# One stationary tile for gate and up of the shared expert, and a SiLU that writes to other partitions

## The chip, the cores and the metric

The kernel runs on one core of one Trainium2 chip. The metric is the device time of one execution in microseconds (us). The kernel before takes 1531.22 us, the median of three runs from 1531.09 to 1531.66.

## The reference, cut to what matters

A macaron block on x of shape (8, 512, 128), all in fp32:

```
x = x + 0.5 * ffn(layernorm(x))
x = x + (layernorm(x) + attention(layernorm(x)))
x = x + 0.5 * ffn(layernorm(x))

ffn(h):      # the same weights both times
    routed   = sum over e of cw[t,e] * ((silu(h @ w_gate[e]) * (h @ w_up[e])) @ w_down[e])   # 32 experts, 64 hidden each
    shared   = (silu(h @ shared_w_gate) * (h @ shared_w_up)) @ shared_w_down                 # 64 hidden
    anchor   = the same form, 16 anchors with 32 hidden each, one anchor per token
    return routed + shared + 0.1 * anchor
```

The combine weights `cw` come from a sigmoid router with a top-2 choice of groups and a top-6 choice of experts. The kernel computes all experts densely and multiplies by `cw`.

## The kernel before

The 4096 tokens are cut into 8 chunks of 512. Each of the two feed-forward blocks (`ffn`, here FFN 1 and FFN 2) goes through the 8 chunks, so there are 16 chunks in all. The hidden columns of all experts (2048), anchors (512) and the shared expert (64) are laid side by side and cut into `HT` = 21 tiles of 128. Tile 20, the last, holds only the 64 columns of the shared expert; its other 64 columns are zeros, in the gate weights, the up weights and the down rows.

For each tile j of a chunk g:

- TensorE (`gate_up`, from L361) multiplies the 128 weight columns by the 512 tokens into one PSUM bank for gate (`psG`) and one for up (`psU`). An fp32 product is made of three matmuls with fp32r halves (`mm3`, L196 to L198: hi by hi, hi by lo, lo by hi), so a tile takes three matmuls for gate and three for up. Every one has a moving operand of 512 columns.
- ScalarE (L725) writes `silu` of the gate bank to SBUF, one of two buffers.
- VectorE (L1069) multiplies it by the up bank into `gated`, one of three buffers, and then (L1097) by the combine weights of the tile's experts, spread over the partitions by a DMA, into `z`. For tile 20 the second step is a plain multiplication by 0.5 (L1100), into a `z` buffer of its own.
- TensorE (`down`, L374) multiplies the rows of `w_down` by `z` and accumulates over the 21 tiles in one bank. It is a plain fp32 matmul, which the trace shows as two records. It runs `LAG` = 3 tiles behind: `down` of tile 17 follows `gate_up` of tile 20, and those of tiles 18, 19 and 20 follow `gate_up` of tiles 0, 1 and 2 of the next chunk.

Each engine runs its own instruction list in a fixed, hand-written order, and semaphores join them. Around the end of a chunk TensorE's order is: `gate_up` 19, `down` 16, `gate_up` 20, `down` 17, `gate_up` 0 of the next chunk, `down` 18, `gate_up` 1, `down` 19, four transposes of the next normalised chunk (`prep_xT`, L336, which wait for `xn_ready`), `gate_up` 2, `down` 20. `gate_up` of a tile waits for `gated` of the tile three before. VectorE's order is: `gated` 19, in FFN 1 the row statistics of a finished chunk (L905, L907), `z` 19, `gated` 20, in FFN 1 the mean and variance (L913 to L919), `z` 20, the normalisation of the chunk after next (`normalise`, L924), `gated` 0, `z` 0. In the first chunk of each FFN a Newton step for the reciprocal standard deviation (`finish_std`, L884 to L895) stands between `z` 20 and the normalisation, and ScalarE computes the square root for it after `silu` 20.

After the last chunk of FFN 1 TensorE does `down` 18 and 19, then waits for `a_xT_lo` (VectorE, L1132, which stands behind `z` 20), projects keys and queries of the first attention pair, and only then does `down` 20. After the last chunk of FFN 2 it does `down` 18, 19 and 20 in a row, and then the chunk's output is copied, transposed, added and stored.

The weights are loaded once, in three groups of seven tiles, and split into their halves by ScalarE (L703) and GpSimd (L1267).

Of the kernel before, what the change touches and what calls it, by code (L numbers as in the profile page):

```python
# [23 lines left out]
ALU = mybir.AluOpType  # L24
# [44 lines left out]
def build(nc, x_in, wg_in, wu_in, wd_in, gate_in, bias_in, wq_in, wk_in, wv_in, wo_in,  # L69
# [6 lines left out]
    with ctx:  # L76
        def sb(name, shape, dt=F32):
            return ctx.enter_context(nc.sbuf_tensor(name, shape, dt))
# [15 lines left out]
        gate_w = sb("gate_w", [P, E])  # L94
        bias = sb("bias", [P, E])
        wg = [sb(f"wg_{n}", [P, HC], F32R) for n in ("hi", "lo")]
        wu = [sb(f"wu_{n}", [P, HC], F32R) for n in ("hi", "lo")]
        wd = sb("wd", [P, HC])
        stage = sb("stage", [P, 2, 3, GT * P])
        stage_flat = stage[:, :, :, :].rearrange("p a b c -> p (a b c)")  # L100
# [125 lines left out]

        ROUTE = 37

        def pair(b, p):

            return b * HP + p
# [25 lines left out]
        @block.sync  # L257
        def _(sp):
            def load_group(sp, k):
                cols = slice(k * GT * P, (k + 1) * GT * P)  # L260
                for w, src in enumerate((wg_in, wu_in)):
                    sp.dma_start(stage[:, k % 2, w, :], src[:, cols]).then_inc(w_loads[k], 16)
                sp.dma_start(wd[:, cols], wd_in[:, cols]).then_inc(w_loads[k], 16)

            def load_x(sp, c):
                sp.dma_start(x[:, c * TB:(c + 1) * TB, :],
                             x_in[c * CH:(c + 1) * CH, :].rearrange("(t p) d -> p t d", p=P)) \
                    .then_inc(x_loads[c], 16)

            sp.dma_start(small[:, :], small_in).then_inc(s["consts_loaded"], 16)  # L270
            load_x(sp, 0)
            sp.dma_start(gate_w[:, :], gate_in).then_inc(s["consts_loaded"], 16)
            sp.dma_start(bias[:, :], bias_in.partition_broadcast(P)).then_inc(s["consts_loaded"], 16)
            load_group(sp, 0)
            load_x(sp, 1)
            load_group(sp, 1)
            for c in range(2, NC):
                load_x(sp, c)
            for k in range(2, W_GROUPS):

                sp.wait_ge(wsplit[k - 2], 2)
                load_group(sp, k)

            def spread_weights(g, first, store=None, after_attention=False):

                sp.wait_ge(s["cwT_sb"], g + 1)
                rows = cw_rows[bass.ds((g % 2) * ROWS, ROWS), :] if not isinstance(g, int) else \
                    cw_rows[(g % 2) * ROWS:(g % 2 + 1) * ROWS, :]
                sp.dma_start(rows, cwT[:, :]).then_inc(s["cw_stored"], 16)
                sp.wait_ge(s["cw_stored"], 16 * (g + 1))  # L290
                if after_attention:
                    sp.wait_ge(s["out_ps"], NC * HP)
                for j in range(SPREAD_TILES):
                    if not (first and j < NSPREAD):
                        sp.wait_ge(s["z_done"], g * HT + j + 1 - NSPREAD - (1 if j < NSPREAD else 0))
                    n = P // (MI if j < E * MI // P else AI)
                    row = j * 2 if j < E * MI // P else E + (j - E * MI // P) * n
                    row = (g % 2) * ROWS + row
                    src = cw_rows[row:row + n, :] if isinstance(g, int) else \
                        cw_rows[bass.ds(row, n), :]  # L300
                    sp.dma_start(spread[:, j % NSPREAD, :],
                                 src.unsqueeze(0).broadcast_to([P // n, n, CH])) \
                        .then_inc(spread_loads[j % NSPREAD], 16)
                    if j == 11 and store is not None:
                        store_chunk(store)

            def store_chunk(c):

                sp.wait_ge(s["x_added"], (c + NC) + 1)
                sp.dma_start(out[bass.ds(c * CH, CH), :].rearrange("(t p) d -> p t d", p=P),  # L310
                             x[:, bass.ds(c * TB, TB), :]).then_inc(s["stored"], 16)

            spread_weights(0, True)

            for k in range(W_GROUPS):
                sp.wait_ge(wsplit[k], 2)
            for w, src in enumerate((wq_in, wk_in)):
                sp.dma_start(attn_w[:, w, :], src).then_inc(s["attn_w_loaded"], 16)
            sp.dma_start(wo[:, :].rearrange("p (j d) -> p j d", d=P),
                         wo_in.rearrange("(j p) d -> p j d", p=P)).then_inc(s["attn_w_loaded"], 16)  # L320
            sp.dma_start(attn_w[:, 2, :], wv_in).then_inc(s["attn_w_loaded"], 16)
            with sp.Fori(1, NC) as g:
                spread_weights(g, False)
            spread_weights(NC, False, after_attention=True)
            with sp.Fori(NC + 1, 2 * NC) as g:
                spread_weights(g, False, g - 1 - NC)
            store_chunk(NC - 1)
            sp.wait_ge(s["stored"], 16 * NC)
# [3 lines left out]
        def _(pe):  # L332
# [24 lines left out]
            def gate_up(g, j, first):  # L357
                if j == 0:
                    pe.wait_ge(s["xT_lo"], g + 1)
                if not (first and j < 3):  # L360
                    pe.wait_ge(s["gated_done"], tiles(g, j) - 3)  # L361
                c = slice(j * P, (j + 1) * P)
                xp = [of_chunk(t, g) for t in xT_parts]
                mm3(pe, psG[j % 3], [w[:, c] for w in wg], xp, True, True)
                mm3(pe, psU[j % 3], [w[:, c] for w in wu], xp, True, True) \
                    .then_inc(s["gate_up_ps"], 1)

            def down(g, j, first):
                pe.wait_ge(s["z_done"], tiles(g, j))
# [298 lines left out]
        def _(act):  # L668
# [28 lines left out]

            def split_hi(k, ws=range(2)):
                act.wait_ge(w_loads[k], 48)
                c = slice(k * GT * P, (k + 1) * GT * P)  # L700
                for w in ws:
                    dst = (wg, wu)[w]
                    nc.scalar.activation(dst[0][:, c], stage[:, k % 2, w, :], ACT.Copy) \  # L703
                        .then_inc(wsplit_hi[k], 1)

            def ffn_chunk(g, first, last, std_n=None):
                for j in range(HT):
                    if std_n == 2 and j in SPLIT_LAST:
                        split_hi(2, (SPLIT_LAST.index(j),))
                    if j == XT + 2 and not last:  # L710
                        prep_copy(g + 1)
                    if j == CWT + 1 and not last:
                        prep_cwT(g + 1)
                    if j == LOGITS + 1 and not last:
                        prep_sigmoid(g + 1)
                    if std_n == 3 and j == 12:
                        row_std(3)
                    if std_n == 3 and j >= AW_SLOT and j - AW_SLOT < 3:
                        attn_split_hi(j - AW_SLOT)
                    if std_n == 3 and j == HT - 1:  # L720
                        a_xT_high(0, psM)
                    act.wait_ge(s["gate_up_ps"], tiles(g, j))
                    if not (first and j < 2):
                        act.wait_ge(s["gated_done"], two_ago(g, j))
                    nc.scalar.activation(silu[j % 2], psG[j % 3], ACT.Silu) \  # L725
                        .then_inc(s["silu_done"], 1)
                    if j == 2 and not first:
                        y_copy(g - 1)
                if first:
                    row_std(std_n)  # L730
# [147 lines left out]
        def _(dve):  # L878
# [181 lines left out]
            def ffn_chunk(g, g0, first, last):  # L1060
# [3 lines left out]
                for j in range(HT):  # L1064
                    if j == 0 and not last:
                        dve.wait_ge(s["xT_ps"], g + 1)
                        normalise(g + 1 - g0, "xn_ready")
                    dve.wait_ge(s["silu_done"], tiles(g, j))
                    tt(gated[j % 3], psU[j % 3], silu[j % 2], ALU.mult) \  # L1069
                        .then_inc(s["gated_done"], 1)  # L1070
                    if j == 9 and not first:
                        add_y(g - 1, g0)
                    if j == XT + 3 and not last:
# [23 lines left out]
                        tt(z[part_slot(j)], gated[j % 3], spread[:, j % NSPREAD, :], ALU.mult) \  # L1097
                            .then_inc(s["z_done"], 1)
                    else:
                        nc.vector.tensor_scalar(z[part_slot(j)], gated[j % 3], 0.5, None, ALU.mult) \  # L1100
                            .then_inc(s["z_done"], 1)
                if before_attention:
                    a_xT_low(0, psM)
# [142 lines left out]
            normalise(0, "xn_ready")  # L1246
            nc.vector.tensor_copy(half[:, :], small[:, P:7 * P])
            nc.vector.memset(cw[:, :, ROWS:], 0.0)
            xT_low(0)
            for k in ROUTING:  # L1250
                ROUTING[k](0)
# [9 lines left out]
        @block.gpsimd  # L1261
        def _(pool):
            def split_lo(k, w):
                c = slice(k * GT * P, (k + 1) * GT * P)
                dst = (wg, wu)[w]
                pool.wait_ge(wsplit_hi[k], w + 1)
                nc.gpsimd.tensor_tensor(dst[1][:, c], stage[:, k % 2, w, :], f32(dst[0][:, c]),  # L1267
                                        ALU.subtract).then_inc(wsplit[k], 1)

            for w in range(2):  # L1270
# [79 lines left out]
```

## Time and profile before

| | |
|---|---|
| median of three runs | 1531.22 us |
| the profiled execution's own time | 1531.53 us |
| span of its trace, first to last instruction | 1529.7 us |
| TensorE busy | 1457.3 us, 95% of the span |
| VectorE busy | 1072.6 us, 70% |
| ScalarE busy | 813.9 us, 53% |
| GpSimd busy | 293.5 us, 19% |
| mean granted clock of TensorE | 0.994 of full speed |

FFN 1 takes the span from about 33 to 432 us, attention from there to about 1129 us, and FFN 2 the rest. A line of the timeline gives the start, the duration, the engine, the line of the kernel, and the operation. Records of matmuls overlap: the duration of one includes its way through the array, and the next starts before it ends. What a matmul takes from the next is the distance between their starts. VectorE's and ScalarE's records can overlap by a little as well.

### The profile page before, as it was taken

What the parts mean: (1) busy time and instruction counts of PE and PEld (TensorE: products, weight loads), DVE (VectorE), ACT (ScalarE), POOL (GpSimd) and SP (SyncE); (2) the same over time, 40 slices, a digit from 0 to 9 for tenths busy, and PEclk for the clock granted to TensorE, in tenths of its full rate; (3) what the DMA queues carried; (4) which work ended last, traced back from release to release, by engine and by line L of the source; (5) the groups of instructions that cost most, each with busy time, mean ns of one, the idle gap of its engine ahead of it and who ended that gap; (6) DMA issues with size and microseconds to landing.
All of it is one profiled execution on the core that took longest, in us unless ns stands there. A gap on an engine that the chain in (4) does not pass through costs nothing.

```text
span 1529.7 us, 29784 instructions
## 1 busy us (share of the span) xinstructions
PE 1457.3 (95%) x9664; PEld 973.4 (64%) x9664; DVE 1072.6 (70%) x2413; ACT 813.9 (53%) x1912; POOL 293.5 (19%) x589
## 2 busy tenths in 40 slices
PE   2999999999989999999999999999889999999998
PEld 1666666666655666665666666666556666666665
DVE  6977877788666666666666575666568777777775
ACT  3444333433457777777777677777743344333422
POOL 2100000000114434334344344344310000000000
PEclk9999999999999999999999999999999999999999
DMA  5443333333300000000000000000023333333333
GB/s 180 130 164 110 106 103 113 105 112 95 113 21 1 1 2 2 2 1 3 2 2 1 3 1 3 1 1 1 1 72 107 111 126 103 118 105 123 106 122 85
DMA packets 58867, 97.94 MB, mean 64 GB/s; under 512 B 6144, under 2 KB 15360, under 8 KB 58752
## 3 DMA queue, kind: packets, MB, share of 16 engines
q1 hardware_dynamic: 58752, 96.44, 19.9%
q8 instruction: 68, 1.11, 0.3%
q14 instruction: 47, 0.39, 0.1%
HBM read 92.75 MB, written 3.67 MB: 63 GB/s over the span
## 4 chain that ended last, share of the span: by engine, by line
PE 49%; issue 30%; POOL 16%; DVE 4%; DMA 1%; ACT 0%; POOLq 0%; SPq 0%; DVEq 0%
PE banks L374 17%; POOL work L1291 16%; PE banks L196 9%; PE banks L198 9%; PE banks L197 9%; PE banks L336 1%; PE banks L346 1%; DVE work L1097 1%; DVE work L1069 1%; PE banks L503 0%; POOL pool_pace L1286 0%; DVE bn L907 0%; DMA bias<-in_gate_bias 0%; DMA work<-cw_rows 0%; POOL aw_lo L1280 0%
## 5 line engine op out<-in xcount | busy, mean ns | idle before, releaser
L725 ACT ACTIVATE work<-banks 128x512 f32<-128x512 f32 x336 | 200.5, 597 | 462.4 <-PE banks L198 444.2
L374 PE MATMUL banks<-work,wd 128*128 128x512 f32 x672 | 342.9, 593 | 0.3 <-DVE work L1097 0.3
L1069 DVE TENSOR_TENSOR work<-banks,work 128x512 f32<-128x512 f32 x336 | 231.9, 690 | 153.0 <-ACT work L725 148.1
L780 ACT ACTIVATE work<-banks,nmax 128x512 f32<-128x512 f32 (+3 forms) x512 | 263.7, 526 | 39.3 <-DVE nmax L1153 39.2
L1291 POOL TENSOR_SCALAR work<-work,rrec 128x512 f32<-128x512 f32 (+3 forms) x512 | 261.6, 533 | 1.6
L196 PE MATMUL banks<-xT_hi,wg_hi 128*128 (+1 forms) x336 | 247.9, 738 | 0.0
L1097 DVE TENSOR_TENSOR work<-work 128x512 f32<-128x512 f32 x320 | 225.7, 705 | 15.8 <-DVE work L1069 9.3
L1168 DVE COPY stage<-banks 128x1024 f32<-128x1024 f32 (+1 forms) x128 | 122.0, 953 | 128.0 <-PE banks L489 128.0
L1153 DVE TENSOR_REDUCE nmax<-banks 128x2 f32<-128x1024 f32 (+3 forms) x256 | 196.0, 808 | 6.4 <-PE banks L478 6.3
L374 PEld LDWEIGHTS banks<-work,wd 128*128 128x128 f32 x672 | 126.3, 189 | 33.4 <-issue 2.2
L196 PE MATMUL banks<-xT_hi,wu_hi 128*128 (+1 forms) x336 | 133.3, 397 | 0.0
L197 PE MATMUL banks<-xT_lo,wg_hi 128*128 (+1 forms) x336 | 133.3, 397 | 0.0
L198 PE MATMUL banks<-xT_hi,wu_lo 128*128 (+1 forms) x336 | 133.3, 397 | 0.0
L197 PE MATMUL banks<-xT_lo,wu_hi 128*128 (+1 forms) x336 | 133.3, 397 | 0.0
L198 PE MATMUL banks<-xT_hi,wg_lo 128*128 (+1 forms) x336 | 133.1, 396 | 0.0
L791 ACT ACTIVATE stage<-banks 128x512 f32<-128x512 f32 x128 | 76.5, 597 | 105.0 <-PE banks L489 105.0
L489 PE MATMUL banks<-small,work 64*128 64x64 f32 x2560 | 111.6, 223 | 3.0 <-DVE stage L1168 2.4
L468 PE MATMUL banks<-k_hi,q_hi 64*128 64x256 f32 (+2 forms) x512 | 102.3, 396 | 8.0 <-ACT work L780 4.2
L196 PEld LDWEIGHTS banks<-xT_hi,wg_hi 128*128 128x128 f32 x336 | 64.1, 191 | 66.7 <-issue 63.8
L197 PEld LDWEIGHTS banks<-xT_lo,wg_hi 128*128 128x128 f32 x336 | 64.5, 192 | 65.2 <-issue 64.8
L780 ACT ACTIVATION_READ_ACCUMULATOR work<-banks,nmax 128x1 f32 x512 | 105.3, 206 | 0.0
L1142 DVE SCALAR_TENSOR_TENSOR q_lo<-banks,q_hi 128x512 fp32r<-128x512 f32 x64 | 44.3, 692 | 85.5 <-ACT q_hi L758 85.4
(122 smaller groups left out, 2215.0 us busy)
## 6 DMA issues: line engine op xcount, KB each, us to landing
work<-cw_rows SPq DMA_DIRECT2D x320, 256.0 KB, 3.1
x<-in_x SPq DMA_DIRECT2D x8, 256.0 KB, 7.0
out_rows<-x SPq DMA_DIRECT2D x8, 256.0 KB, 2.2
cw_rows<-cwT SPq DMA_DIRECT2D x16, 96.0 KB, 1.9
stage<-in_w_gate SPq DMA_DIRECT2D x3, 448.0 KB, 5.7
stage<-in_w_up SPq DMA_DIRECT2D x3, 448.0 KB, 6.4
wd<-in_w_down SPq DMA_DIRECT2D x3, 448.0 KB, 7.3
stage<-in_wq SPq DMA_DIRECT2D x1, 512.0 KB, 3.8
```

Of the source, the lines that this page charges most:

```text
L196: pe.matmul(o, w[0], m[0], start=start, stop=False, skip_group_check=True)
L197: pe.matmul(o, w[0], m[1], start=False, stop=False, skip_group_check=True)
L198: return pe.matmul(o, w[1], m[0], start=False, stop=stop, skip_group_check=True)
L374: pe.matmul(psY, wd[:, j * P:(j + 1) * P], z[part_slot(j)], start=j == 0, stop=j == HT - 1, skip_group_check=True).then_inc(s["down_ps"], 1)
L489: m = pe.transpose(psT[:, h, k * DK:(k + 1) * DK], prob[r, p % 2, i, o:o + P], ident[r, h * DK:(h + 1) * DK])
L725: nc.scalar.activation(silu[j % 2], psG[j % 3], ACT.Silu) \
L780: m = nc.scalar.activation(prob[:, p % 2, i, o:o + w], ps[:, i, so:so + w], ACT.Exp, bias=nmax[:, p % 2, i, qb:qb + 1], accum_out=rsum[:, ...
L1069: tt(gated[j % 3], psU[j % 3], silu[j % 2], ALU.mult) \
L1097: tt(z[part_slot(j)], gated[j % 3], spread[:, j % NSPREAD, :], ALU.mult) \
L1153: m = nc.vector.tensor_reduce(nmax[:, p % 2, :, qb], ps[:, :, o:o + (qb + 1) * P], AX.X, ALU.max, negate=True)
L1168: nc.vector.tensor_copy(*transposed(p, g, slice(0, 2 - g))).then_inc(s["pT_dve"], 1)
L1291: nc.gpsimd.tensor_scalar(t, t, rrec[:, par, i, qb:qb + 1], 1.0, ALU.mult, ALU.mult) \
```

## The change

The shared expert's up columns move into the 64 free columns of the gate weights of tile 20. The three gate matmuls of tile 20 then give 64 gate rows (partitions 0 to 63) and 64 up rows (partitions 64 to 127) in one bank, and the three up matmuls of tile 20 are gone. ScalarE reads partitions 0 to 63 of the bank and writes the SiLU to partitions 64 to 127 of its buffer; VectorE multiplies it by the up rows on partitions 64 to 127, and scales them by 0.5 there. The down rows of the shared expert move to the upper half of their tile, and the lower half of the `z` buffer is set to zero once at the start. The up weights are one tile narrower, so the third group's load and split of the up weights cover six tiles, not seven.

```diff
-        wu = [sb(f"wu_{n}", [P, HC], F32R) for n in ("hi", "lo")]
+        wu = [sb(f"wu_{n}", [P, HC - P], F32R) for n in ("hi", "lo")]
...
+        def split_columns(k, w):
+
+            return slice(k * GT * P, min((k + 1) * GT, HT - w) * P)
...
                 for w, src in enumerate((wg_in, wu_in)):
-                    sp.dma_start(stage[:, k % 2, w, :], src[:, cols]).then_inc(w_loads[k], 16)
+                    c = split_columns(k, w)
+                    sp.dma_start(stage[:, k % 2, w, 0:c.stop - c.start], src[:, c]).then_inc(w_loads[k], 16)
...
-                mm3(pe, psG[j % 3], [w[:, c] for w in wg], xp, True, True)
-                mm3(pe, psU[j % 3], [w[:, c] for w in wu], xp, True, True) \
-                    .then_inc(s["gate_up_ps"], 1)
+                m = mm3(pe, psG[j % 3], [w[:, c] for w in wg], xp, True, True)
+                if j < HT - 1:
+                    m = mm3(pe, psU[j % 3], [w[:, c] for w in wu], xp, True, True)
+                m.then_inc(s["gate_up_ps"], 1)
...
-                    nc.scalar.activation(silu[j % 2], psG[j % 3], ACT.Silu) \
-                        .then_inc(s["silu_done"], 1)
+                    if j < HT - 1:
+                        nc.scalar.activation(silu[j % 2], psG[j % 3], ACT.Silu) \
+                            .then_inc(s["silu_done"], 1)
+                    else:
+                        nc.scalar.activation(silu[j % 2][MI:, :], psG[j % 3][0:MI, :], ACT.Silu) \
+                            .then_inc(s["silu_done"], 1)
...
-                    tt(gated[j % 3], psU[j % 3], silu[j % 2], ALU.mult) \
-                        .then_inc(s["gated_done"], 1)
+                    if j < HT - 1:
+                        tt(gated[j % 3], psU[j % 3], silu[j % 2], ALU.mult) \
+                            .then_inc(s["gated_done"], 1)
+                    else:
+                        tt(gated[j % 3][MI:, :], psG[j % 3][MI:, :], silu[j % 2][MI:, :], ALU.mult) \
+                            .then_inc(s["gated_done"], 1)
...
-                        nc.vector.tensor_scalar(z[part_slot(j)], gated[j % 3], 0.5, None, ALU.mult) \
+                        nc.vector.tensor_scalar(z[part_slot(j)][MI:, :], gated[j % 3][MI:, :], 0.5, None,
+                                                ALU.mult) \
                             .then_inc(s["z_done"], 1)
...
             nc.vector.memset(cw[:, :, ROWS:], 0.0)
+            nc.vector.memset(z[part_slot(HT - 1)][0:MI, :], 0.0)
             xT_low(0)
```

The rest of the diff passes the narrower column ranges to the two splits and lays out the weights on the host.

## Rows read from the trace of the kernel before

**Rows 1.** The page: busy time of each engine and its share of the span.
```profile
PE 1457.3 (95%) x9664; PEld 973.4 (64%) x9664; DVE 1072.6 (70%) x2413; ACT 813.9 (53%) x1912; POOL 293.5 (19%) x589
```

**Rows 2.** Windows: length, busy time of PE, PEld, DVE, ACT, POOL; clock; DMA.
```profile
180.00:240.00 60.00, 60.00 (x229) 40.78 (x227) 46.05 (x127) 22.96 (x35) 0.00 (x0) 1.00 0.34 112
...
1220.00:1280.00 60.00, 60.00 (x229) 40.79 (x228) 44.40 (x105) 23.27 (x36) 0.00 (x0) 1.00 0.35 112
```

**Rows 3.** Waits of the span: total us, times, longest us.
```profile
PE banks L336 <- DVE xn L924: 12.4, 2, 11.5
```

**Rows 4.** The page's groups: last up matmul; busy us, mean ns, idle before.
```profile
L198 PE MATMUL banks<-xT_hi,wu_lo 128*128 (+1 forms) x336 | 133.3, 397 | 0.0
```

**Rows 5.** Timeline of TensorE, FFN 1, tile 20 of a middle chunk, and the next transposes.
```profile
231.43 0.39 PE L196 MATMUL banks<-xT_hi,wu_hi 128*128 x1
...
231.89 0.39 PE L198 MATMUL banks<-xT_hi,wu_lo 128*128 x1
232.12 1.02 PE L374 MATMUL banks<-work,wd 128*128 128x512 f32 x2
...
237.50 0.60 PE L336 MATMUL banks<-small,xn 128*128 128x128 f32 x4
```

**Rows 6.** Timeline of VectorE at the same boundary, from z 19 on.
```profile
232.15 0.67 DVE L1097 TENSOR_TENSOR work<-work 128x512 f32<-128x512 f32 x1
232.95 0.69 DVE L1069 TENSOR_TENSOR work<-banks,work 128x512 f32<-128x512 f32 x1
...
234.34 0.43 DVE L1100 TENSOR_SCALAR work<-work 128x512 f32<-128x512 f32 x1
235.11 1.12 DVE L924 TENSOR_SCALAR xn<-x,mean,rstd 128x128 f32 x4 [0.34 <-issue]
```

**Rows 7.** Timeline from the first to the second chunk of FFN 1.
```profile
84.05 0.69 DVE L1097 TENSOR_TENSOR work<-work 128x512 f32<-128x512 f32 x1
...
84.65 0.69 DVE L1069 TENSOR_TENSOR work<-banks,work 128x512 f32<-128x512 f32 x1
...
87.38 1.13 DVE L924 TENSOR_SCALAR xn<-x,mean,rstd 128x128 f32 x4 [0.51 <-DVE rstd L895]
...
88.67 0.60 PE L336 MATMUL banks<-small,xn 128*128 128x128 f32 x4
```

**Rows 8.** Timeline from FFN 1 to attention.
```profile
429.40 2.74 PE L374 MATMUL banks<-work,wd 128*128 128x512 f32 x6
429.42 0.69 DVE L1097 TENSOR_TENSOR work<-work 128x512 f32<-128x512 f32 x1
...
430.23 0.69 DVE L1069 TENSOR_TENSOR work<-banks,work 128x512 f32<-128x512 f32 x1
...
431.30 0.68 DVE L1132 TENSOR_TENSOR xT_lo<-banks,xT_hi 128x512 fp32r<-128x512 f32 x1
432.04 0.50 PE L196 MATMUL banks<-xT_hi,aw_hi 128*128 128x512 f32 x1
```

**Rows 9.** Timeline of a middle boundary of FFN 2: normalisation and transposes.
```profile
1426.17 1.13 DVE L924 TENSOR_SCALAR xn<-x,mean,rstd 128x128 f32 x4 [0.31 <-issue]
...
1429.26 0.60 PE L336 MATMUL banks<-small,xn 128*128 128x128 f32 x4
```

**Rows 10.** Timeline of the end of FFN 2: down 17 to 20, and z 20.
```profile
1521.35 3.60 PE L374 MATMUL banks<-work,wd 128*128 128x512 f32 x8
...
1522.90 0.43 DVE L1100 TENSOR_SCALAR work<-work 128x512 f32<-128x512 f32 x1
```

**Rows 11.** Timeline: a ScalarE copy on 48 partitions, and VectorE's idle time at the start.
```profile
228.75 0.59 ACT L692 ACTIVATE cwT<-banks 48x512 f32<-48x512 f32 x1 [0.78 <-PE banks L336]
...
13.82 0.69 DVE L1050 TENSOR_TENSOR xT_lo<-xT,xT_hi 128x512 fp32r<-128x512 f32 x1 [1.52 <-ACT xT_hi L678]
```

**Rows 12.** Windows at the end of attention, columns as in rows 2.
```profile
1113.00:1121.00 8.00, 7.34 (x50) 3.32 (x48) 3.34 (x19) 0.81 (x2) 4.07 (x9) 0.57 0.00 1
1121.00:1128.00 7.00, 5.99 (x46) 2.84 (x40) 4.01 (x10) 2.84 (x6) 0.00 (x0) 1.00 0.01 2
```

More of the change, by code:

```diff
@@ L699, in split_hi @@
                 act.wait_ge(w_loads[k], 48)
-                c = slice(k * GT * P, (k + 1) * GT * P)
                 for w in ws:
+                    c = split_columns(k, w)
                     dst = (wg, wu)[w]
-                    nc.scalar.activation(dst[0][:, c], stage[:, k % 2, w, :], ACT.Copy) \
+                    nc.scalar.activation(dst[0][:, c], stage[:, k % 2, w, 0:c.stop - c.start], ACT.Copy) \
                         .then_inc(wsplit_hi[k], 1)
@@ L1263, in split_lo @@
             def split_lo(k, w):
-                c = slice(k * GT * P, (k + 1) * GT * P)
+                c = split_columns(k, w)
                 dst = (wg, wu)[w]
                 pool.wait_ge(wsplit_hi[k], w + 1)
-                nc.gpsimd.tensor_tensor(dst[1][:, c], stage[:, k % 2, w, :], f32(dst[0][:, c]),
+                nc.gpsimd.tensor_tensor(dst[1][:, c], stage[:, k % 2, w, 0:c.stop - c.start], f32(dst[0][:, c]),
                                         ALU.subtract).then_inc(wsplit[k], 1)
@@ L1317, in hidden_columns @@
         parts = [interleave(w).transpose(3, 0, 1, 2).reshape(D, -1) for w in (experts, anchors)]
-        parts.append(np.asarray(shared))
-        w = np.zeros((D, HT * P), np.float32)
-        w[:, :sum(p.shape[1] for p in parts)] = np.concatenate(parts, 1)
-        return w
+        return np.concatenate(parts + [np.asarray(w) for w in shared], 1)
     down = np.zeros((HT * P, D), np.float32)
@@ L1325 @@
                            interleave(np.asarray(L0_ffn_anchor_w_down).transpose(0, 2, 1)).reshape(-1, D),
+                           np.zeros((P - MI, D), np.float32),
                            np.asarray(L0_ffn_shared_w_down)], 0)
-    down[:rows.shape[0]] = rows
+    down[:, :] = rows
     arrays = {
         "x": x.reshape(B * S, D),
-        "w_gate": hidden_columns(L0_ffn_w_gate, L0_ffn_anchor_w_gate, L0_ffn_shared_w_gate),
-        "w_up": hidden_columns(L0_ffn_w_up, L0_ffn_anchor_w_up, L0_ffn_shared_w_up),
+        "w_gate": hidden_columns(L0_ffn_w_gate, L0_ffn_anchor_w_gate,
+                                 [L0_ffn_shared_w_gate, L0_ffn_shared_w_up]),
+        "w_up": hidden_columns(L0_ffn_w_up, L0_ffn_anchor_w_up, []),
         "w_down": down.reshape(HT, P, D).transpose(1, 0, 2).reshape(P, HT * D),
```

## The prediction, on record before the changed kernel was run

> **What bounds the kernel now.** I read the busy times first [rows 1]: TensorE is busy for 95% of the span, VectorE for 70%. A share of busy time says nothing about a stage, so the windows came next [rows 2]. In both FFNs TensorE is busy for 60.00 of 60 us, at the full granted clock (2.4 GHz), with VectorE at 46.05 and 44.40 and ScalarE at 23. The table of waits [rows 3] holds the control: TensorE waited twice for the normalised rows, 12.4 us in all, and both waits stand at the start of an FFN (11.5 of it before the first chunk; the rest is the start of FFN 2). Inside the FFNs TensorE sets the pace, and what leaves its list there shortens the time, as long as the next engine keeps up. Attention has its own pattern, which the change does not touch.
>
> **The removed matmuls.** Three matmuls go in each of 16 chunks, 48 in all. The row that groups them gives a mean of 397 ns [rows 4]; 48 of those would be 19.1 us. That number is the trap: the records overlap. The price is the distance from one start to the next, (231.89 - 231.43)/2 = 0.23 us, and the same again from the last of them to the down matmul at 232.12 [rows 5]. Three are 232.12 - 231.43 = 0.69, with rounding 0.70 us per chunk. All 16 would give 11.2 us; that is the upper end if every chunk boundary hands its 0.70 us on.
>
> The Trainium skill ("TensorE: Matmul & The Clock Gate", section "Back-to-back issue gap") gives N/2.4 + 2.5 ns, 216 ns for 512 columns, for a single gap, and says that a sustained stream of loads and matmuls comes to about 131 ns at 512 columns. By the second, 14 boundaries would give 14 x 3 x 0.131 = 5.5 us. The row shows 0.23 us in this very stream, so I keep the row.
>
> **Does each boundary hand it on?** TensorE now reaches everything behind tile 20 earlier by 0.70 us. Its next wait with a producer near is the one of the four transposes for the normalised rows. The producer is VectorE, and VectorE does not move by 0.70 us: its `gated` 20 stands behind `z` 19, which hangs on tile 19.
>
> Middle boundaries of FFN 1: `z` 19 ends at 232.15 + 0.67 = 232.82 and `gated` 20 starts at 232.95 [rows 6], so an earlier SiLU brings VectorE forward by 0.13 us only. The normalised rows are done at 235.11 + 1.12 = 236.23, then 236.10. TensorE wants them at 237.50 [rows 5], then at 236.80. 0.7 us of slack are left, less the hand-over. Nothing is lost; these are the ends of chunks 1 to 5. After chunk 6 no transposes follow, and `down` 17 to 20 wait for `z` values that are 2 us old or more.
>
> Middle boundaries of FFN 2 have no statistics between: rows done at 1426.17 + 1.13 = 1427.30, wanted at 1429.26 [rows 9], then 1428.56. Nothing is lost. The first boundary of FFN 2 has VectorE waiting for the SiLU, so its whole chain moves along with TensorE. At the end of FFN 2 the last down matmul starts about 2.6 us behind 1521.35 and `z` 20 is done at 1522.90 + 0.43 = 1523.33 [rows 10]; moved by 0.70 the matmul would start at 1523.2, but `z` 20 comes earlier too by up to 0.70, as VectorE idled before `gated` 20. The chunk pays in full. So 6 boundaries of FFN 1 and 8 of FFN 2 pay 0.70 us: 9.8 us.
>
> Two boundaries don't.
> - Chunk 0 to 1 of FFN 1. VectorE goes from `z` 19 at 84.05 straight to `gated` 20 at 84.65 and on to the normalisation, which ends at 87.38 + 1.13 = 88.51; TensorE takes the rows at 88.67 [rows 7]. It would come at 87.97 and wait. The hand-over from VectorE to TensorE took 0.06 us where rows 8 show one (431.98 to 432.04), so TensorE starts at 88.57 to 88.67: gain 0 to 0.10, I take 0.05.
> - FFN 1 to attention. Three down matmuls end at about 429.40 + 2.6 = 432.0, and `xT_lo`, behind `gated` 20 and `z` 20, ends at 431.98 [rows 8]. They tie. TensorE would come at 431.3. VectorE's `z` 19 starts at 429.42; with the spacing of 0.60 that the pair in rows 7 has, `gated` 20 starts at 430.03 instead of 430.23. So the projection starts 0.20 us earlier at most; I take 0.15. What follows (keys, queries, scores) is a chain from that start.
>
> **The operations on 64 partitions.** Before has no VectorE operation of this kind. The nearest row is ScalarE's copy of 48 x 512 with 0.59 us [rows 11], beside 0.60 us for a full 128 x 512 SiLU: time goes by the elements of one partition, so SiLU, product and scaling keep their 0.60, 0.69 and 0.43 us. That is my value. The lower end is half of each, by the number of partitions; it would free VectorE by (0.69 + 0.43)/2 = 0.56 us at the two tight boundaries, up to 1.0 us more in all. The upper end, a doubling for the new placing, is the third rival below. Smaller: a VectorE instruction starts before the one ahead has ended (start distance 0.60 against 0.69 us [rows 7]). If one on other partitions had to wait for that end, `gated` 20 and the instruction behind `z` 20 would each be late by 0.09 us, together 0.18 us at each tight boundary, -0.3 us in all, and nothing where there is slack. The Trainium skill states just that ("VectorE: DVE Perf Modes", section "Two Vector instructions with no wait between them"): an instruction whose start quadrant differs from the one last used starts only when all earlier ones have finished. By that rule the sum would be 9.7 us; no row here shows it.
>
> **Edits at nothing.** The memset of 64 x 512 falls into 1.52 us in which VectorE waits for ScalarE before its first `xT_lo` [rows 11]; without that cover it would cost its own length, about 0.5 us. The narrower third load and split save 1/7 of one split on ScalarE and GpSimd, dozens of us before tile 14 needs them. No DMA is added, no queue is passed, and the new instructions wait for the same semaphores as the old; the spread weights of the next chunk hang on tile 18, not 20. `gate_up` 2 of the next chunk needs `gated` 20, done at about 233.6, and would start at 237.2.
>
> **Sum.** 9.8 + 0.05 + 0.15 = 10.0 us. From the profiled execution's 1531.53 that is 1521.5 us; from the median of 1531.22 it is 1521.2. The 0.3 us between them is the spread of the runs; with the 0.3 us by which held VectorE starts would reduce the gain, the median comes to 1521.5 as well. I predict 1521.5.
>
> **The rivals.**
> 1. All of it pays: VectorE's work shrinks with the partitions, or the two ties are softer than they look. 16 x 0.70 = 11.2: 1520.2. Against it is the 48-partition row.
> 2. Removing three matmuls returns only two distances, because the load of the down weights used to run beside them and now has less cover. The distance 0.23 us is then paid back at every boundary: 14 x 0.46 = 6.4 plus about 0.2: 1524.8. Against it: behind the three gate matmuls stands the same down matmul with the same neighbour in front of it. The number 397 ns taken at its word, 1512.4, has nothing for it.
> 3. VectorE becomes the bound at more boundaries: the operations on the upper half cost twice, 1.12 us more before the normalisation. In FFN 1 the rows are done at 236.10 + 1.12 = 237.2 against 236.80 wanted, and with the hand-over those five boundaries keep about 0.2 us each (1.0); the two tight ones lose 1 us each (-2.0); the first of FFN 2 breaks even; the other eight pay in full (5.6). Gain 4.6: 1526.9. A smaller surcharge, 0.4 us, would cost only the two tight ones 0.4 us each: 1522.3.
> 4. Slower. At the end of attention TensorE's granted clock is 0.57 over 8 us, between stretches at 1.00 [rows 12]: it idles there in pieces and falls to 1.2 GHz. The work now comes at other moments against whatever grants the clock, and the two new waits of TensorE at tight boundaries are idle pieces too. It decides against the change if low stretches grow by 20 us of busy TensorE, each microsecond at half rate losing 0.5 us, so that 10 us are gone: 1532 or more. For it: the stretch of rows 12 exists. Against it: it has (1 - 0.57) x 2 x 8 = 7 us at the low level, and three such would have to be added while the order of work in attention stays as it is; the new waits are 0.6 us in a stretch with the clock at 1.00.
>
> **How the numbers follow.** Forecast 0.80 (own range 1520.8 to 1522.4), rival 1 0.05, rival 2 0.04, rival 3 0.07, rival 4 0.03, the remaining 0.01 for no change. The range of 8 in 10 reaches from rival 1 with the spread of the runs, 1519.9, to short of rivals 2 and 3, 1523.6. No change is within 0.2%, 3 us, which is about what a measurement here can tell: faster 0.95 (all cases but rival 4 and the rest), same 0.02, slower 0.03.
>
> **What would show it.** In the trace after, tile 20 has three matmuls before its down matmul, and the distance from the last one of tile 20 to the first of tile 0 stays; a middle chunk of either FFN takes 0.70 us less; the transposes of the second chunk of FFN 1 have a new wait for L924 of about 0.6 us, and the first projection one for `xT_lo` of about 0.5 us; SiLU, product and scaling of tile 20 keep their lengths; attention takes as long as before. It is wrong if a middle chunk saves other than 0.65 to 0.75 us, if the middle boundaries show a wait of TensorE, or if attention's length moves by more than 1 us.

## The result, and the profile after

The changed kernel takes 1521.99 us, the median of four runs from 1519.59 to 1523.24; before, 1531.15 us with four runs. The ratio is 0.9939, with a 95% interval from 0.9922 to 0.9957; this and the ratios below compare the means of all runs, and so differ a little from the quotient of two medians. The profiled execution took 1522.03 us with a span of 1520.3 us. Forecast was 1521.5 us.

Below is the page of the kernel after: busy times, and the groups of the last gate and the last up matmul. Against [rows 1] and [rows 4] the up group has 320 instructions where 336 stood, its mean duration is 396 against 397 ns, and TensorE's busy time fell by 11.2 us.

```profile
PE 1446.1 (95%) x9616; PEld 963.9 (63%) x9616; DVE 1074.4 (71%) x2414; ACT 813.8 (54%) x1912; POOL 293.2 (19%) x589
...
L198 PE MATMUL banks<-xT_hi,wg_lo 128*128 (+1 forms) x336 | 133.2, 396 | 0.0
...
L198 PE MATMUL banks<-xT_hi,wu_lo 128*128 (+1 forms) x320 | 126.7, 396 | 0.0
```

TensorE stays busy through both FFNs, as in [rows 2] (windows of the kernel after, same columns):

```profile
180.00:240.00 60.00, 60.00 (x228) 40.62 (x227) 47.45 (x129) 23.69 (x36) 0.00 (x0) 1.00 0.38 112
1220.00:1280.00 60.00, 60.00 (x228) 40.62 (x227) 45.35 (x106) 24.31 (x38) 0.00 (x0) 1.00 0.38 120
```

A middle boundary of FFN 1 in the timeline after. It answers to [rows 5, 6]. The down matmul (L380) comes 0.23 us behind the last gate matmul of tile 20. The SiLU on 64 partitions takes 0.59 us, the product 0.69, the scaling 0.42. The normalised rows end at 234.57 + 1.12 = 235.69 and TensorE takes them at 236.22, in its own time: 0.53 us of slack. At the five middle boundaries of FFN 1 it is 0.47 to 0.53 us.

```profile
230.62 0.40 PE L198 MATMUL banks<-xT_hi,wg_lo 128*128 x1
...
230.85 1.02 PE L380 MATMUL banks<-work,wd 128*128 128x512 f32 x2
231.05 0.59 ACT L735 ACTIVATE work<-banks 64x512 f32<-64x512 f32 x1 [0.96 <-PE banks L198]
...
231.58 0.67 DVE L1111 TENSOR_TENSOR work<-work 128x512 f32<-128x512 f32 x1
...
232.28 0.69 DVE L1083 TENSOR_TENSOR work<-banks,work 64x512 f32<-64x512 f32 x1
...
233.91 0.42 DVE L1114 TENSOR_SCALAR work<-work 64x512 f32<-64x512 f32 x1
...
234.57 1.12 DVE L934 TENSOR_SCALAR xn<-x,mean,rstd 128x128 f32 x4 [0.24 <-issue]
...
236.22 0.60 PE L341 MATMUL banks<-small,xn 128*128 128x128 f32 x4
```

The two tight places. First the boundary of chunks 0 and 1, which answers to [rows 7], then the entry to attention, which answers to [rows 8]. Both now show a wait of TensorE, 0.67 and 0.62 us, for VectorE: the normalised rows end at 88.28 + 1.12 = 89.40 and the transposes start at 89.47; `xT_lo` ends at 428.60 and the projection starts at 428.65.

```profile
84.71 0.68 DVE L1111 TENSOR_TENSOR work<-work 128x512 f32<-128x512 f32 x1
...
85.42 0.69 DVE L1083 TENSOR_TENSOR work<-banks,work 64x512 f32<-64x512 f32 x1
...
86.15 0.42 DVE L1114 TENSOR_SCALAR work<-work 64x512 f32<-64x512 f32 x1
...
86.61 0.30 DVE L894 RECIPROCAL rstd<-std 128x24 f32<-128x24 f32 x1
...
88.28 1.12 DVE L934 TENSOR_SCALAR xn<-x,mean,rstd 128x128 f32 x4 [0.51 <-DVE rstd L905]
89.44 0.69 DVE L1080 TENSOR_TENSOR work<-banks,work 128x512 f32<-128x512 f32 x1
89.47 0.66 PE L341 MATMUL banks<-small,xn 128*128 128x128 f32 x4 [0.67 <-DVE xn L934]
...
426.00 0.69 DVE L1111 TENSOR_TENSOR work<-work 128x512 f32<-128x512 f32 x1
426.72 0.69 DVE L1083 TENSOR_TENSOR work<-banks,work 64x512 f32<-64x512 f32 x1
427.45 0.42 DVE L1114 TENSOR_SCALAR work<-work 64x512 f32<-64x512 f32 x1
427.91 0.69 DVE L1147 TENSOR_TENSOR xT_lo<-banks,xT_hi 128x512 fp32r<-128x512 f32 x1
428.65 0.50 PE L196 MATMUL banks<-xT_hi,aw_hi 128*128 128x512 f32 x1 [0.62 <-DVE xT_lo L1147]
```

**Where the time came from.** ScalarE copies the combine weights once per chunk, behind tile 18 of the chunk before, as soon as TensorE has transposed them. The start of that copy marks the chunks. The table gives the time between consecutive marks, and for each stretch the time after minus the time before. The last stretch ends at the start of the last addition (L1057 before, L1067 after).

| stretch | before, us | after - before, us |
|---|---|---|
| start to the mark ahead of chunk 0 | 33.88 | +0.95 |
| chunk 0 up to tile 18 | 45.95 | -0.29 |
| over boundary 0 to 1 of FFN 1 | 49.70 | +0.19 |
| over boundaries 1 to 2 ... 5 to 6 of FFN 1 | 49.61 each | -0.71, -0.71, -0.72, -0.71, -0.71 |
| over boundary 6 to 7, to the first projection | 54.45 | -0.68 |
| first projection to the mark at the end of attention | 694.66 | -0.34 |
| chunk 0 of FFN 2 up to tile 18 | 45.67 | -0.09 |
| over boundaries 0 to 1 ... 5 to 6 of FFN 2 | 49.68, then 49.62 each | -0.68, -0.71, -0.72, -0.72, -0.72, -0.70 |
| the rest, over two chunk ends | 56.27 | -1.42 |

Fourteen chunk ends pay about 0.71 us each, 9.9 us (the stretch with -0.68 holds one of them and 0.03 us lost at the entry to attention). I take the start to be no part of the change: the transfer that VectorE's first instruction waits for landed at 7.42 us before and 8.38 after, and anywhere from 6.98 to 9.14 us in the kernels below, while no transfer ahead of it was changed. The -0.09 in the first chunk of FFN 2 is spread too: it is -0.01 or 0.00 in every kernel below.

### The profile page after: what moved, and what is told of

It reads as the page before. It is cut to its first block, busy times and chain, and to the rows that moved or that the text cites. A ratio compares the mean times of both kernels' runs of the same rounds, so it can differ in the third digit from the quotient of the medians.

```text
span 1520.3 us, 29689 instructions
## 1 busy us (share of the span) xinstructions
PE 1446.1 (95%) x9616; PEld 963.9 (63%) x9616; DVE 1074.4 (71%) x2414; ACT 813.8 (54%) x1912; POOL 293.2 (19%) x589
## 4 chain that ended last, share of the span: by engine, by line
PE 80%; DVE 11%; ACT 4%; issue 3%; DMA 1%; DVEq 0%; SPq 0%; ACTq 0%
PE banks L380 17%; PE banks L196 13%; PE banks L198 11%; PE banks L197 11%; PE banks L509 9%; PE banks L474 7%; PE banks L495 5%; PE banks L522 3%; DVE stage L1183 2%; PE banks L484 2%; DVE nmax L1168 2%; ACT work L790 2%; PE banks L341 2%; DVE work L1080 1%; DVE work L1111 1%
## 5 line engine op out<-in xcount | busy, mean ns | idle before, releaser
L732 ACT ACTIVATE work<-banks 128x512 f32<-128x512 f32 x320 | 191.0, 597 | 433.2 <-PE banks L198 421.0
L380 PE MATMUL banks<-work,wd 128*128 128x512 f32 x672 | 342.6, 593 | 0.1
L1080 DVE TENSOR_TENSOR work<-banks,work 128x512 f32<-128x512 f32 x320 | 220.6, 689 | 140.1 <-ACT work L732 135.2
L380 PEld LDWEIGHTS banks<-work,wd 128*128 128x128 f32 x672 | 126.3, 189 | 33.1 <-DVE work L1111 1.9
L196 PE MATMUL banks<-xT_hi,wu_hi 128*128 (+1 forms) x320 | 126.9, 397 | 0.0
L197 PE MATMUL banks<-xT_lo,wu_hi 128*128 (+1 forms) x320 | 126.9, 396 | 0.0
L198 PE MATMUL banks<-xT_hi,wu_lo 128*128 (+1 forms) x320 | 126.7, 396 | 0.0
```

The costliest lines, as they stand in the source:

```text
L196: pe.matmul(o, w[0], m[0], start=start, stop=False, skip_group_check=True)
L197: pe.matmul(o, w[0], m[1], start=False, stop=False, skip_group_check=True)
L198: return pe.matmul(o, w[1], m[0], start=False, stop=stop, skip_group_check=True)
L380: pe.matmul(psY, wd[:, j * P:(j + 1) * P], z[part_slot(j)], start=j == 0, stop=j == HT - 1, skip_group_check=True).then_inc(s["down_ps"], 1)
```

## The experiments

Executions of one kernel differ by up to 7 us here, so the verdicts rest on the marks and waits of the traces, which repeat to about 0.03 us inside the FFNs; the timed runs are a check on the sum. Runs that are given against the same time of the kernel before stood beside the same runs of it.

**The changed kernel again.** 

> The changed kernel again, beside the others on the same chip and in more rounds. Theory (14 boundaries pay 0.71 us each, the first boundary of FFN 1 and the entry to attention pay nothing): 9.9 us less than before from the matmuls, so a ratio of about 0.9935. Rival (the 1.0 us by which the changed kernel's first transfers landed later, 8.38 against 7.42 us, belongs to the change): the start is late again by 1.0 us. By the theory it falls either way, as the transfers before it are the same.

Measured: 1522.92 us against 1532.57, ratio 0.9929 (0.9917 to 0.9941). The steps are those of the table (-0.29 became -0.26; +0.19, -0.71 to -0.72, -0.68), the waits 0.7 and 0.6 us. The start was +0.58 this time. The steps at the boundaries repeat.

**Halves swapped.**

```diff
-    nc.scalar.activation(silu[j % 2][MI:, :], psG[j % 3][0:MI, :], ACT.Silu)
+    nc.scalar.activation(silu[j % 2][0:MI, :], psG[j % 3][MI:, :], ACT.Silu)
-    tt(gated[j % 3][MI:, :], psG[j % 3][MI:, :], silu[j % 2][MI:, :], ALU.mult)
+    tt(gated[j % 3][0:MI, :], psG[j % 3][0:MI, :], silu[j % 2][0:MI, :], ALU.mult)
...   # the scaling, the memset and the weights alike
```

> The halves are swapped: up rows on partitions 0 to 63, gate rows on 64 to 127, ScalarE writes the SiLU to the lower 64, and VectorE works on partitions 0 to 63. Theory (VectorE holds an instruction back until the one ahead has ended when it starts on other partitions): the distances z 19 to product 20 and scaling 20 to the next instruction, 0.71 and 0.46 us in the changed kernel's tight places, go back to 0.60 and 0.34, and each of the two tight boundaries gains 0.23 us, 0.5 us in all against the changed kernel. Rival (a half-height instruction costs this whatever its place): distances and time stay as they are. Between middle boundaries neither theory expects a difference.

Measured: 1521.94 us, ratio 0.9926 (0.9913 to 0.9939), on the same chip as the one above; that difference is inside both intervals. The timeline of this kernel, at the two tight places, decides:

```profile
84.68 0.68 DVE L1111 TENSOR_TENSOR work<-work 128x512 f32<-128x512 f32 x1
85.28 0.68 DVE L1083 TENSOR_TENSOR work<-banks,work 64x512 f32<-64x512 f32 x1
85.99 0.42 DVE L1114 TENSOR_SCALAR work<-work 64x512 f32<-64x512 f32 x1
86.33 0.29 DVE L894 RECIPROCAL rstd<-std 128x24 f32<-128x24 f32 x1
...
428.10 0.50 PE L196 MATMUL banks<-xT_hi,aw_hi 128*128 128x512 f32 x1 [0.37 <-DVE xT_lo L1147]
```

The product follows its forerunner by 0.60 us, not 0.71, the reciprocal the scaling by 0.34, not 0.46. The instructions are as high as before and as long; only their first partition is 0 now. The step over boundary 0 to 1 went from +0.19 to -0.07, the wait at the projection from 0.62 to 0.37. In the changed kernel both start 0.03 to 0.04 us behind the end of the one ahead (85.39 and 85.42, 86.57 and 86.61), here 0.08 us ahead of it. So a VectorE instruction is held until the one ahead has ended when it starts on partition 64 where partition 0 was used last, or the other way round. The Trainium skill ("VectorE: DVE Perf Modes", section "Two Vector instructions with no wait between them") states this as a rule for groups of 32 partitions, kept for the inputs and the output, and for SBUF and PSUM separately. The traces agree, at 0.11 to 0.12 us per held instruction.

A third instruction is held, and it shows that the one directly ahead does not decide. `gated` 0 of the next chunk follows the normalisation, which works on all partitions from SBUF, by 1.16 us in the changed kernel (88.28 to 89.44), by 1.04 here (87.99 to 89.03) and by 1.04 before (87.38 to 88.42). The last instruction that had read a PSUM bank ahead of it was product 20, on partitions 64 to 127. In the first chunk of FFN 1, where no product 20 has run yet, the distance is 1.03 us in the changed kernel too. TensorE waits for none of this.

**Six matmuls kept.**

```diff
-                if j < HT - 1:
-                    m = mm3(pe, psU[j % 3], [w[:, c] for w in wu], xp, True, True)
+                cu = slice(min(j, HT - 2) * P, (min(j, HT - 2) + 1) * P)
+                m = mm3(pe, psU[j % 3], [w[:, cu] for w in wu], xp, True, True)
```

> The changed kernel with the three up matmuls of tile 20 put back as idle work (they multiply tile 19's up weights into the bank that nobody reads). This leaves the half-height instructions alone. Theory (the gain is the matmuls' only): as before within 0.5 us, with the two tight boundaries late by up to 0.2 us each: ratio to before 1.000. Rival (part of the gain comes from elsewhere, the bank that VectorE reads or the half-height work): 1 us or more below before.

Measured: 1532.97 us against 1532.57, ratio 1.0000 (0.9991 to 1.0009). All middle steps are within 0.01 of zero; the boundary 0 to 1 is +0.20 and the entry +0.13. The whole gain at a middle boundary is the matmuls', and the half-height work costs nothing there. The first chunk was 0.28 us shorter even here, which the theory did not have; see the wide split below.

**One matmul in tile 20.** The two low-order products of the gate tile are left out.

```diff
-                m = mm3(pe, psG[j % 3], [w[:, c] for w in wg], xp, True, True)
+                if j < HT - 1:
+                    m = mm3(pe, psG[j % 3], [w[:, c] for w in wg], xp, True, True)
+                else:
+                    m = pe.matmul(psG[j % 3], wg[0][:, c], xp[0], start=True, stop=True,
+                                  skip_group_check=True)
```

> Tile 20 keeps only its hi by hi matmul of gate; the two low-order products are left out, so the output loses precision there. Theory (a matmul is worth its start distance of 0.235 us, and middle boundaries of FFN 1 have 0.53 us of slack for the normalised rows): two fewer, 0.47 us, still pay in full at 14 boundaries, 6.6 us less than the changed kernel, and nothing at the two tight ones; the transposes of the middle boundaries come within 0.1 us of the rows. Rival (the duration of 0.397 us is the worth): 11.1 us less. Rival (the slack is smaller than read): the five middle boundaries of FFN 1 pay less than 0.47 and show waits of TensorE for the rows.

Measured: 1517.15 us against 1532.57, ratio 0.9890 (0.9876 to 0.9904). The steps in FFN 2 are -1.16 to -1.18 (one -1.14), so two more matmuls are worth 0.46 us: 0.23 each, the start distance and not the duration of 0.40. At the five middle boundaries of FFN 1 they are -1.05 to -1.13, so the two matmuls pay 0.34 to 0.41 there and not 0.46, and the transposes start 0.05 to 0.08 us behind the end of the rows, as at a tight place. The second rival is right by that much: less the hand-over of 0.06 us, the slack that TensorE can use is 0.41 to 0.47 us and not 0.53. The duration as a price (11.1 us less than the changed kernel) falls; measured are 5.8.

**The product twice.**

```diff
+        spare = sb("spare", [P, CH])
...
                     else:
+                        tt(spare[MI:, :], psG[j % 3][MI:, :], silu[j % 2][MI:, :], ALU.mult)
                         tt(gated[j % 3][MI:, :], psG[j % 3][MI:, :], silu[j % 2][MI:, :], ALU.mult)
```

> The changed kernel with the product of tile 20 done once more on VectorE, into a spare buffer: 0.61 us more of VectorE's time ahead of scaling 20 in every chunk, nothing else. Theory (slack as read from the changed kernel's trace: 0.47 us at the middle boundaries of FFN 1, about 0.4 at the first of FFN 2, over 1 us at the others of FFN 2, none at the first of FFN 1 and at the entry to attention): TensorE waits 0.14 us at each of the five middle boundaries of FFN 1, 0.2 at the first of FFN 2, 0.61 more at each of the two tight places, nothing elsewhere; 2.1 us more than the changed kernel. Rival (VectorE's work at a boundary is hidden everywhere, its 70% says so): no change. Rival (VectorE is late at all boundaries): 16 x 0.61 = 9.8 us more.

Measured: 1525.19 us against 1531.15, ratio 0.9948 (0.9935 to 0.9962). Two rows of TensorE's waits in this kernel:

```profile
PE banks L342 <- DVE xn L935: 13.9, 4, 11.1
...
PE banks L197 <- DVE xT_lo L1149: 1.2, 1, 1.2
```

Of the four waits in the first row the longest stands ahead of the first chunk, and the one at boundary 0 to 1 is 1.27 us (0.67 in the changed kernel). The wait at the projection grew from 0.62 to 1.21 us, the step over boundary 0 to 1 from +0.19 to +0.79: 0.6 us at each tight place. The middle boundaries of FFN 1 pay 0.47 to 0.53 instead of 0.71, a loss of 0.18 to 0.24 where 0.14 was expected: the 0.61 us of the product less 0.4 us of usable slack. FFN 2 lost nothing, also at its first boundary, where I had expected 0.2. There VectorE waits 0.36 us for ScalarE's square root behind `z` 20 in the changed kernel; the extra product fills that wait and takes the rest from the slack, which falls from 0.47 to 0.19 us. VectorE's room is a matter of the place: none, 0.4 us, or more than 0.6.

**Two moves.** In the changed kernel:

```diff
-            FIRST_STATS = dict(zip((2, 3, 4, 6, 9, 19), range(2, NC)))
+            FIRST_STATS = dict(zip((2, 3, 4, 6, 9, 18), range(2, NC)))
...
+                    if before_attention and j == HT - 1:
+                        a_xT_low(0, psM)
                     dve.wait_ge(s["silu_done"], tiles(g, j))
...
-                    a_xT_low(0, psM)
...
-                    pe.wait_ge(s["gated_done"], tiles(NC - 1, HT - 1))
+                    pe.wait_ge(s["gated_done"], tiles(NC - 1, HT - 2))
```

> The changed kernel with VectorE's list relieved at the two tight places: in the first chunk the statistics of the eighth chunk's rows go from tile 19 to tile 18, and at the end of FFN 1 xT_lo is computed ahead of product 20 (the first projection's other wait then needs product 19 only, the last reader of its banks). Theory (those two places kept their 0.71 us because VectorE was late): TensorE's waits of 0.67 and 0.62 us there vanish and the kernel gains 1.3 us against the changed one. Rival (something else is next, the spread weights or ScalarE's square root and table loads): the waits go to another releaser and less than 0.5 us is gained.

Measured: 1520.13 us against 1531.15, ratio 0.9919 (0.9905 to 0.9932). The step over boundary 0 to 1 is -0.72. At the entry, in the timeline of this kernel, `xT_lo` ends at 427.15 and the projection follows the down matmuls without a wait. The record of its first matmul now starts while the down matmul ahead still runs (0.80 us long, not 0.50), so from here on I take the second matmul of the projection as the mark. The stretch from the last copy to it is 0.89 us shorter than in the changed kernel, more than the wait of 0.62.

```profile
426.46 0.69 DVE L1148 TENSOR_TENSOR xT_lo<-banks,xT_hi 128x512 fp32r<-128x512 f32 x1
...
427.33 0.80 PE L196 MATMUL banks<-xT_hi,aw_hi 128*128 128x512 f32 x1
```

**The same moves in the kernel before.** The same edits, but the projection waits for product 20 still. 

> The kernel before with the same two moves and nothing of the change (the projection still waits for product 20, whose bank it takes). Theory (the places became tight by the change, before they tied to within 0.1 us): no gain, within 0.2 us of before by the steps from chunk to chunk. Rival (they held the kernel up already): 0.5 us or more is gained.

Measured: 1532.70 us against 1531.15, ratio 1.0012 (1.0001 to 1.0023). All steps inside the FFNs are -0.01 to +0.01 against before, and the entry gained 0.16 us. So `xT_lo` had been a little late already: the "tie" of [rows 8] was a loss of 0.16 us. The 0.89 us are then the 0.71 that this chunk end should have paid, the 0.03 that it had lost instead, and these 0.16. The ratio lies just above 1 with nothing in the steps to go with it; the spread of attention would cover it, but that is not shown.

**Moves and swapped halves.** 

> Both moves and the swapped halves together, the version that should be the fastest. Theory (the held starts of VectorE cost only where it is late, and the moves have made room): within 0.1 us of the two moves alone, 1.3 us less than the changed kernel, a ratio to before of about 0.9925. Rival (held starts cost at every boundary): 0.2 us or more below the two moves alone at each boundary, 3 us in all.

Measured: 1520.60 us against 1531.15, ratio 0.9921 (0.9907 to 0.9934), beside the two moves alone with 0.9919. The step over boundary 0 to 1 is -0.69. Once the moves have made room the held starts cost nothing, as expected. But the profiled executions of the two kernels with moves had an attention of 696.9 and 696.7 us (from the second matmul of the projection), where the changed kernel had 694.0 and the kernel before 694.3. Was the gain given back there? Both kernels once more, on one chip:

> Both moves and the swapped halves once more, now beside the changed kernel on the same chip, as the two stood on different chips so far. Theory (1.6 us of TensorE's waits and of the tie at the entry to attention are gone): 1.6 us less than the changed kernel beside it, with attention's own length, which went from 693.6 to 697.0 us in the executions profiled so far, adding a spread of about that size. Rival (what is gained ahead of attention is given back in it, since its length was 696.7 and 696.9 us in the two kernels with the moves): attention is 2 us or more longer than in the changed kernel beside it, and the two kernels' medians are equal.

> The changed kernel beside the other two. Theory: steps between chunks of -0.71 us, wait of 0.67 us at the second chunk and 0.62 at the first projection as before; attention's length anywhere from 693.6 to 697. Rival (attention is always 693.9 to 694.3 us in this kernel, so its length belongs to the kernel): 694 us again.

Measured: 1519.80 us with the moves, 1520.55 without, against 1531.20; ratios 0.9921 (0.9906 to 0.9936) and 0.9931 (0.9912 to 0.9949). Attention took 693.4 us with the moves this time and 694.6 without. It is not given back: the same kernel had 696.7 and 693.4 us, and two kernels without the moves, the one with one matmul and the one with the product twice, had 696.1 and 697.0. One thing that differs between the two executions of the same kernel is the granted clock. Windows of the kernel with moves and swapped halves, first execution:

```profile
1100.00:1123.00 23.00, 18.13 (x154) 9.36 (x153) 14.21 (x52) 8.97 (x25) 8.05 (x17) 0.85 0.00 1
```

and in the second, where TensorE was busy as long with the clock at 0.93 instead of 0.85:

```profile
1100.00:1123.00 23.00, 18.07 (x160) 9.99 (x159) 13.55 (x52) 9.02 (x22) 5.62 (x13) 0.93 0.02 6
```

Added up in windows of 20 us over all of attention, the clock was at its low level for about 18 us in the first execution and 10 in the second. But the kernel before had about 17 us of it and took only 694.3 us, so the length of the low stretches alone does not set the time of attention. Its cause stays open.

The two kernels with moves have the lowest steps and neither wait. At the two tight places together they are 1.8 us below the changed kernel by the traces. The timed runs of the last comparison side with this, 0.8 us apart in the medians, but their intervals overlap, so that the kernels with moves beat the changed kernel is shown by the traces and not by the times.

**The wide split.** The changed kernel with the up weights padded to 21 tiles.

```diff
-        wu = [sb(f"wu_{n}", [P, HC - P], F32R) for n in ("hi", "lo")]
+        wu = [sb(f"wu_{n}", [P, HC], F32R) for n in ("hi", "lo")]
...
-            return slice(k * GT * P, min((k + 1) * GT, HT - w) * P)
+            return slice(k * GT * P, (k + 1) * GT * P)
```

> The changed kernel with the up weights as wide as before (a tile of zeros at the end that no matmul reads), so that the third group's loads and splits cover seven tiles again. In all kernels with the narrower split the first chunk was 0.26 to 0.29 us shorter, also where the six matmuls were kept. Theory (VectorE's multiplication by the combine weights ends 0.55 us after GpSimd's split that runs beside it, so a shorter split, 2.27 instead of 2.56 us, frees VectorE earlier): the split takes 2.56 us again, the product beside it 1.88 instead of 1.60, and the time from the first to the second chunk's combine weights is back at 45.95 us. Rival (the shorter loads or ScalarE's shorter split are the cause, or it is spread): that time stays at 45.67. The rest of the trace as in the changed kernel: 0.28 us slower than it.

Measured: 1523.40 us, ratio 0.9947 (0.9929 to 0.9965). The first chunk up to tile 18 took 45.95 us, to the hundredth the time before; the other steps stayed. The timeline of the changed kernel, GpSimd's split and VectorE's product beside it,

```profile
41.84 2.27 POOL L1283 TENSOR_TENSOR wu_lo<-stage,wu_hi 128x768 fp32r<-128x768 f32 x1
...
43.06 1.60 DVE L1111 TENSOR_TENSOR work<-work 128x512 f32<-128x512 f32 x1
```

and of the kernel with the wide split:

```profile
41.72 2.56 POOL L1283 TENSOR_TENSOR wu_lo<-stage,wu_hi 128x896 fp32r<-128x896 f32 x1
...
42.96 1.88 DVE L1111 TENSOR_TENSOR work<-work 128x512 f32<-128x512 f32 x1
```

The product alone takes 0.69 us. Beside the split it ends 0.55 us behind the split's end, 44.66 and 44.11, or 44.84 and 44.28. This kernel widens the loads, ScalarE's split and GpSimd's together, so the time by itself does not tell them apart. The lines do: in both kernels the product starts 1.22 to 1.24 us behind the start of GpSimd's split, and its duration alone carries the 0.28 us. The shorter split of GpSimd is the cause.

## Why the prediction was right, step by step

- The price of a removed matmul, 0.23 us from start to start and not 0.40: right. The steps are 0.71 us for three, and in FFN 2 the one-matmul kernel gives 0.46 for two.
- Fourteen boundaries pay in full, two don't: right in number and in place, 9.9 us against 9.8. The six-matmul kernel shows that nothing else pays there.
- The slack at the middle boundaries of FFN 1: mis-sized, 0.7 us less the hand-over of 0.06 against 0.47 to 0.53 less the same. The text let the earlier SiLU bring VectorE forward by 0.13 us and kept the held starts for the tight places. They come at every boundary: with the halves swapped the slack in the same chunk is 0.79 us. It did not matter for the change, as TensorE waits at none of the five.
- The gain at boundary 0 to 1, +0.05: the term that failed, -0.19 us. The text had priced the held starts at 0.18 us per tight place and left them out of the base sum as not shown. They happen, at 0.11 and 0.12 us per instruction; with the halves swapped the place gains 0.07 us, where 0.05 was forecast.
- The gain at the entry to attention, +0.15: missed too, it is -0.03 us. The held starts again take it away (0.23 us are gained with the halves swapped), and the tie of before was not quite one.
- The operations on 64 partitions keep their length: right, 0.59, 0.69 and 0.42 us.
- Edits at nothing: the memset (0.48 us) lies in VectorE's wait and costs nothing. The narrower split was costed at nothing and gives 0.28 us. I had looked for who waits for the split's data, not for who is held up by it while it runs.
- Attention as long as before: within the 1 us that was set, 0.34 us less, inside its own spread. No rival came true. The fourth, the clock, named a possible source of the 3 us of spread in attention, which no run tested; it never came near 10 us.

The sum of the terms is 9.9 + 0.28 + 0.34 + 0.09 - 0.19 = 10.4 us behind the start, and the later start takes 0.95 of it from this one execution. That the total came within 0.5 us of the forecast is in part luck. The two tight places gave 0.4 us less than forecast, the split and attention 0.6 us more, and the medians of three comparisons of these two kernels lie 9.2, 9.7 and 10.7 us apart. The steps at the boundaries bear the prediction out, not the closeness of the total.

## What to carry to other kernels

Price a removed matmul by the distance between starts, and count the places at which the engine that comes next is already late: a saving ahead of such a place is worth only what that engine can follow. When a step is cheapened that "nobody waits for", look also at what runs slower beside it. Two equal operands side by side in one half-empty stationary tile paid here because ScalarE could bring the halves together at no extra time; put the halves so that VectorE stays on the start partition of its neighbours.

## What the runs showed of the hardware that was not expected

- A VectorE product with two SBUF inputs, started beside a GpSimd `tensor_tensor` of 128 x 896, took 1.88 us instead of 0.69, and 1.60 beside one of 128 x 768; both ended 0.55 us behind the end of the GpSimd instruction. A product with one input in PSUM took its usual 0.68 us beside the same instruction.
- An instruction of VectorE that starts on other partitions than were used last starts 0.11 us later behind a product (0.71 against 0.60) and 0.12 us later behind the scaling (0.46 against 0.34). For one that reads PSUM the last reader of PSUM counted, even with a normalisation from SBUF between them (1.16 against 1.04 us).
- ScalarE read partitions 0 to 63 of PSUM and wrote 64 to 127 of SBUF, and the other way round, at the price of a full 128 x 512 SiLU, 0.59 against 0.60 us.
- Attention of one and the same kernel took 693.4 and 696.7 us in two executions, with the granted clock from 1100 to 1123 us at 0.93 and 0.85. Why the clock falls differently was not tried, nor whether it makes the difference.
